# A direct path for the first query stacks, and products of ones on TensorE, at the start of two attention layers

## What is computed

```python
    def _L1_xattn_ref(Q, K, V, Wq, bq, Wk, bk, Wv, bv, Wo, bo):
...
        q = proj(Q, Wq, bq)
        k = proj(K, Wk, bk)
        v = proj(V, Wv, bv)
        scores = jnp.einsum('bhqd,bhkd->bhqk', q, k) / np.sqrt(Dk)
        attn = jax.nn.softmax(scores, axis=-1)
        out = jnp.einsum('bhqk,bhkd->bhqd', attn, v)
        out = out.transpose(0, 2, 1, 3).reshape(B, -1, D)
        return jnp.einsum('bsd,de->bse', out, Wo.T) + bo
...
    x = x + jnp.tanh(g_xattn[1]) * _L1_xattn_ref(_layernorm(x, axis=-1), ctx_1024, ctx_1024, L1_xattn_Wq, L1_xattn_bq, L1_xattn_Wk, L1_xattn_bk, L1_xattn_Wv, L1_xattn_bv, L1_xattn_Wo, L1_xattn_bo)
```

## Time and profile before

| | |
|---|---|
| three timed executions | 1617.97, 1623.83, 1623.98 us; median 1623.83 |
| the profiled execution | 1621.11 us, of which its span 1619.3 us |
| TensorE matmul busy | 1384.8 us, 86% of the span |
| VectorE, ScalarE, GpSimd busy | 861.7, 547.1 and 418.2 us |
| SyncE's DMA queue q1 | 133.89 MB, 28.4% of 16 engines' span |

### The profile page before, as it was taken

The page is one execution under the profiler, slowest core; times in us unless marked ns, Lnnn a source line. Parts: engine busy times, 40 slices in busy tenths (PEclk is TensorE's granted clock), DMA queues, the critical chain, the costliest instruction groups (busy, mean ns, idle before and its releaser), DMA issues. The chain is left out here.

```text
span 1619.3 us, 26329 instructions
## 1 busy us (share of the span) xinstructions
PE 1384.8 (86%) x8869; PEld 865.7 (53%) x8869; DVE 861.7 (53%) x2507; ACT 547.1 (34%) x1291; POOL 418.2 (26%) x729
## 2 busy tenths in 40 slices
PE   5799886995999859896994994756999999999998
PEld 2577663543787636555883773543444444344343
DVE  5577646874676523323663433754455546446425
ACT  2366555652577622223551331430101011011001
POOL 3687501104777100001344123620000000000000
PEclk9699987995799979995776997887999999999999
DMA  6766730004677468000001111232211302202200
GB/s 181 169 153 150 161 83 1 1 1 106 157 170 178 84 244 354 0 1 27 27 27 36 49 55 43 65 117 105 105 51 61 111 19 93 112 1 110 105 7 13
DMA packets 74720, 143.01 MB, mean 88 GB/s; under 512 B 13430, under 2 KB 53878, under 8 KB 64742
## 3 DMA queue, kind: packets, MB, share of 16 engines
q1 hardware_dynamic: 68038, 133.89, 28.4%
q0 software_dynamic: 3296, 6.76, 1.4%
q10 hardware_dynamic: 3264, 0.79, 0.3%
HBM read 99.33 MB, written 41.09 MB: 87 GB/s over the span
## 5 line engine op out<-in xcount | busy, mean ns | idle before, releaser
L2700 DVE TENSOR_TENSOR l3f_weighted_T<-l3f_w_e,l3f_xnT 128x512 f32<-128x512 f32 x128 | 88.4, 691 | 129.7 <-PE psum L2451 114.5
L2451 PE MATMUL psum<-l3f_weighted_T,w_l3f_q 128*128 128x512 f32 x256 | 133.7, 604 | 16.5 <-DVE l3f_weighted_T L2700 14.7
L2451 PE MATMUL psum<-l3f_weighted_T,w_l3f_k 128*128 128x512 f32 x256 | 131.6, 596 | 0.0
L2451 PE MATMUL psum<-l3f_weighted_T,w_l3f_v 128*128 128x512 f32 x256 | 131.3, 594 | 0.0
L2460 PE MATMUL psum<-l3f_weighted_T,w_l3f_o 128*128 128x512 f32 x256 | 124.3, 624 | 1.7 <-DVE l3f_weighted_T L2700 1.7
L2700 DVE TENSOR_TENSOR l3f_weighted_T<-l3f_w_e,l3f_oT 128x512 f32<-128x512 f32 x128 | 88.4, 692 | 57.2 <-PE psum L2460 30.3
L707 DVE TENSOR_REDUCE l1x_minus_max<-psum 128x4 f32<-128x512 f32 x128 | 84.7, 686 | 61.4 <-PE psum L360 60.5
L707 DVE TENSOR_REDUCE l0x_minus_max<-psum 128x4 f32<-128x512 f32 x128 | 84.4, 686 | 38.6 <-PE psum L360 37.9
L111 POOL TENSOR_TENSOR l3f_ln_rstd<-l3f_ln_mean_var,eps 128x4 f32<-128x4 f32 x8 | 2.0, 245 | 355.8 <-DVE l3f_ln_mean_var L104 355.8
L2460 PEld LDWEIGHTS psum<-l3f_weighted_T,w_l3f_o 128*128 128x128 f32 x256 | 39.3, 188 | 82.8 <-DVE l3f_weighted_T L2700 78.1
L2451 PEld LDWEIGHTS psum<-l3f_weighted_T,w_l3f_v 128*128 128x128 f32 x256 | 48.9, 191 | 61.8 <-issue 61.8
(11 more groups left out here) (486 smaller groups left out, 2991.5 us busy)
## 6 DMA issues: line engine op xcount, KB each, us to landing
l3f_w_e<-l3f_weights_scratch SPq DMA_DIRECT2D x32, 1024.0 KB, 4.7
sorted_x<-zeros SPq DMA_DIRECT2D x1, 16896.0 KB, 59.5
l0x_k_stack<-l0x_k_scratch SPq DMA_DIRECT2D x48, 192.0 KB
l0x_q_stack<-l0x_q_scratch SPq DMA_DIRECT2D x48, 192.0 KB
l1x_k_stack<-l1x_k_scratch SPq DMA_DIRECT2D x48, 192.0 KB
l1x_q_stack<-l1x_q_scratch SPq DMA_DIRECT2D x48, 192.0 KB
w_l2f_w<-in_l2f_w SPq DMA_DIRECT2D x2, 2048.0 KB, 13.2
l0x_k_scratch<-l0x_k_parts SPq DMA_DIRECT2D x16, 192.0 KB, 6.4
```

The costliest lines, as they stand in the source:

```text
L2451: ins = pe.matmul(bank[:, :], w[name][:, e, :], xe[:, e % 2, :], start=(e == 0), stop=(e == NE3 - 1))
L2700: dve.tensor_tensor(xe[:, e % 2, :], wE[:, g % 2, e, :], src, ALU.mult).then_inc(s_xe, 1)
```

## The change

The first halves of the q stacks of the groups 0 and 1 no longer pass through DRAM. `lay_straight` copies each part from `parts` straight to its three places in the stack: 9 transfers of 64 KB, each from 128 partitions (512 bytes of each) to 8 partitions, issued as each part is ready. The second halves still take the way over DRAM, and so do all later groups. The load of group 1's first k half moves ahead of its q.

TensorE gets products of ones (`keep_busy`, 512 columns in float32, the result is never read): two at the start of layer 1, four ahead of the first scores, one after each second set of scores, 14 in layer 1 and 12 in layer 0. The projections of the groups 0 and 1 get PSUM banks of their own and another order; turned maxima 1 and 2, the transposes and the q projection of group 2 move into iteration 0 of the loop, and the other engines' lists follow. x and ctx are loaded in eight pieces of 256 KB instead of three and a rest. In the diff the blocks are, in order, helpers, SyncE's list, TensorE's list (the prelude, then iteration j of the loop), GpSimd's, VectorE's, and the pieces of x and ctx.

```diff
+        def banks_of(n, g):
+            return {("k", 1): bankS, ("q", 1): bankT, ("v", 0): bankT}.get((n, g), [bankP0, bankP1])
+        def xn_bank(g):
+            return bankA if g < 2 else bankP1
...
+            def lay_straight(g):
+                for a in range(NPART):
+                    if a < NPART - 1:
+                        links = 4 if rope else 3
+                        sp.wait_ge(s_first if g == 0 else s_split, links + (2 if rope else 1) + 2 * a)
+                    else:
+                        sp.wait_ge(s_parts["q"], g + 1)
+                    for b in range(NPART):
+                        at = (b * NPART + (a - b) % NPART) * HD
+                        sp.dma_start(stack["q"][at:at + HD, g, 0, :, :], parts["q"][:, a, half(0)])\
+                          .then_inc(s_stack["q"][g][0], 16)
...
-            store("q", 0)
-            load("q", 0, 0)
+            lay_straight(0)
+            store("q", 0, (1,))
             load("q", 0, 1)
             if name == "l0x":
                 k.load_x(sp, 3)
-                k.load_ctx(sp, 3)
             for g in range(1, NG):
                 store("k", g)
-                store("q", g)
-                load("k", g, 0)
-                load("q", g, 0)
+                if g == 1:
+                    load("k", g, 0)
+                    lay_straight(g)
+                    store("q", g, (1,))
+                else:
+                    store("q", g)
+                    load("k", g, 0)
+                    load("q", g, 0)
+                if name == "l0x" and g + 2 < NG:
+                    k.load_ctx(sp, g + 2)
+                if name == "l0x" and g + 3 < NG:
+                    k.load_x(sp, g + 3)
                 load("k", g, 1)
                 load("q", g, 1)
...
+            def keep_busy(n):
+                for _ in range(n):
+                    pe.matmul(bankA[:, :], v1[:, 0, 0, 0:HEADS - 1, :].rearrange("p h d -> p (h d)")[:, 0:P],
+                              v1[:, 0, :, :, :].rearrange("p c h d -> p (c h d)")[:, 0:T], start=True, stop=True)
...
-            for g in range(2):
-                project_k(g)
-                turn_xn(g)
-                project_q(g)
-                project_v(g)
-                if g == 0:
-                    pe.matmul(bankM[:, 0:P], bcast(w["bv"][:, 0:1], [P, P]), w["wo"][:, :], start=True, stop=True).then_inc(s_bp, 1)
+            if not rope:
+                pe.wait_ge(s_fill, 4)
+                keep_busy(2)
+            k.wait_weights(pe, name)
+            pe.wait_ge(s_fill, 4)
+            project_k(0)
+            if not rope:
+                project_k(1)
+                project_v(0)
+            turn_xn(0)
+            if rope:
+                project_v(0)
+            project_q(0)
+            turn_xn(1)
+            if rope:
+                project_k(1)
+            project_q(1)
+            project_v(1)
+            pe.matmul(bankM[:, 0:P], bcast(w["bv"][:, 0:1], [P, P]), w["wo"][:, :], start=True, stop=True).then_inc(s_bp, 1)
+            pe.wait_ge(s_out["k"], 2)
+            keep_busy(4)
             for j in range(LEAD):
                 for u in range(4):
                     scores(j, u)
-                if j >= 1:
-                    turn_max(j - 1)
+                    if u % 2:
+                        keep_busy(1)
                 if j == 1:
-                    project_k(2)
-                if j == 2:
-                    turn_xn(2)
-            project_q(2)
+                    turn_max(0)
+            project_k(2)
+            pe.wait_ge(s_out["q"], 2)
...
                 unit(1)
+                if j == 0:
+                    turn_max(1)
...
                 unit(2)
+                if j == 0:
+                    turn_xn(2)
                 unit(3)
+                if j == 0:
+                    turn_max(2)
                 if j + LEAD - 1 < NSEQ:
                     turn_max(j + LEAD - 1)
+                if j == 0:
+                    project_q(2)
...
-            for g in range(3):
-                moments(g)
+            moments(0)
+            moments(1)
             split("k", 1)
+            moments(2)
+            split_max(0)
             split("q", 1)
-            split_max(0)
             split_max(1)
-            moments(3)
             split_max(2)
             split("k", 2)
+            moments(3)
...
             moments(0)
+            moments(1)
             rotate("k", 0)
             split_first("k")
-            moments(1)
...
-    PIECES = (slice(0, T), slice(T, 2 * T), slice(2 * T, 3 * T), slice(3 * T, NSEQ * P))
+    PIECES = tuple(slice(g * T, (g + 1) * T) for g in range(NG))
```

More of the change, by code:

```diff
@@ L256, in heads_attention, with straight @@
         stores = {"k": 1, "q": 2}
+        def straight(n, g, hf):
+            return n == "q" and g < 2 and hf == 0
         def stack_landed(eng, n, g, hf):
-            eng.wait_ge(s_stack[n][g % 2][hf], 16 * loads[n] * (g // 2 + 1))
+            loaded = loads[n] * (g // 2 + 1)
+            if n == "q" and hf == 0:
+                loaded += NPART * NPART - loads["q"]
+            eng.wait_ge(s_stack[n][g % 2][hf], 16 * loaded)
         def parts_stored(eng, n, g, hf):
-            eng.wait_ge(s_stored[n][hf], 16 * stores[n] * (g + 1))
+            if straight(n, g, hf):
+                stack_landed(eng, n, g, hf)
+            else:
+                through = g + 1 if n == "k" or hf == 1 else g - 1
+                eng.wait_ge(s_stored[n][hf], 16 * stores[n] * through)
         block = ctx.enter_context(nc.Block())
@@ L272, in _, with store @@
                          bcast(ones_row[:, 0:HALF].unsqueeze(1), [NPART, 4 * HEADS, HALF])).then_inc(s_ones, 16)
-            def store(n, g):
+            def store(n, g, halves=(0, 1)):
                 sp.wait_ge(s_parts[n], g + 1)
-                for hf in range(2):
+                for hf in halves:
                     to = scratch[n][g % 2, hf].rearrange("a p t -> p a t")
@@ L332, in turn_xn @@
                 pe.wait_ge(s_xn, g + 1)
-                if rope:
+                if g >= 1:
+                    pe.wait_ge(s_xnT, g)
+                if g >= 2 and rope:
                     pe.wait_ge(s_out["k"], g + 1)
                 for c in range(GS):
-                    ins = pe.transpose(bankP1[:, seq(c)], xn[:, c, :], k.ident[:, :])
+                    ins = pe.transpose(xn_bank(g)[:, seq(c)], xn[:, c, :], k.ident[:, :])
                 ins.then_inc(s_xnP, 1)
             def project_q(g):
-                pe.wait_ge(s_out["k"], g + 1)
+                if g == 1:
+                    pe.wait_ge(s_vout, 1)
+                else:
+                    pe.wait_ge(s_out["k"], g + 1)
                 pe.wait_ge(s_xnT, g + 1)
@@ L344, in project_v @@
             def project_v(g):
-                pe.wait_ge(s_out["q"], g + 1)
+                if g >= 1:
+                    pe.wait_ge(s_out["q"], g + 1 if g > 1 else 1)
+                k.wait_ctx(pe, g)
                 for c in range(GS):
-                    ins = pe.matmul(bankP0[:, seq(c)], k.ctxT[:, seq(g * GS + c)], w["wv"][:, :], start=True, stop=True)
+                    ins = pe.matmul(banks_of("v", g)[0][:, seq(c)], k.ctxT[:, seq(g * GS + c)], w["wv"][:, :],
+                                    start=True, stop=True)
                 ins.then_inc(s_proj["v"], 1)
@@ L533, in _ @@
             act.wait_ge(s_fill, 4)
-            for g in range(2):
-                evacuate("k", g)
-                for c in range(GS):
-                    normalise_x(g, c)
-                xnT_out(g)
-                evacuate("q", g)
-                v_out(g)
+            evacuate("k", 0)
+            for c in range(GS):
+                normalise_x(0, c)
+            if not rope:
+                v_out(0)
+            xnT_out(0)
+            evacuate("q", 0)
+            if rope:
+                v_out(0)
+            for c in range(GS):
+                normalise_x(1, c)
+            evacuate("k", 1)
+            xnT_out(1)
+            evacuate("q", 1)
+            v_out(1)
+            max_out(0)
+            max_rows(0)
             for c in range(GS):
                 normalise_x(2, c)
-            max_out(0)
-            max_rows(0)
             evacuate("k", 2)
-            max_out(1)
-            max_rows(1)
-            xnT_out(2)
-            max_out(2)
-            max_rows(2)
-            evacuate("q", 2)
-            normalise_x(3, 0)
             for j in range(NSEQ + 2):
@@ L558, in _ @@
                     exps(j, 1)
+                if j == 0:
+                    max_out(1)
+                    max_rows(1)
                 if j >= 2:
@@ L564, in _ @@
                     exps(j, 2)
+                if j == 0:
+                    xnT_out(2)
                 if c == 3 and t + 3 < NG:
@@ L568, in _ @@
                     exps(j, 3)
+                if j == 0:
+                    max_out(2)
+                    max_rows(2)
                 if j + LEAD - 1 < NSEQ:
@@ L571, in _ @@
```

(9 more changed lines are left out.)

32 lines of the change are left out of this document (16 added, 16 removed).

## The result

The changed kernel takes 1642.0 us, median, against 1623.9: ratio 1.0114, 95% interval 1.0082 to 1.0146. It is slower, and by 18 us where the forecast said 12. One of its four timed executions, 1667.3 us, was a slow one; it is in the median and not in the ratio. The profiled execution has a span of 1637.3 us against 1619.3.

The account below looks back on a forecast made before the run. Bounds: TensorE in the loops (95 and 99% busy), and at each layer's start the moment group 1's four stack halves are in. Layer 0 +0.4 and layer 1 +11.6 make +12.0 on 1621.1 us: 1633, range 1610 to 1648.

Parts of the forecast that it names:

- Price of a straight half: Nine transfers into 8 partitions each, on SyncE's queue, take 8.0 us, by two readings 6.8 to 9.2.
- the row of ones: Profile row of transfers from SBUF into 3 partitions: 24 GB/s, 8.0 per partition, 14% of 16 DMA engines busy.
- First scores: Start of each layer: layer 0's at 36.4 against 36.22, +0.2; layer 1's 5.0 us later.
- The products' charge of 5.0: Head of layer 1: fill and two products of ones ahead of k's projection, charged at 5.0 us.
- Group 1's half: Group 1's straight half, for which iteration 0 waits, lands at 58.6 in layer 0 and 426.2 in layer 1.
- Iteration 1 at 68.0 instead of 67.63: +0.4: Layer 0's loop: iteration 1 starts when sequence 1's maxima land with the loads ahead of them, 0.4 us later.
- +11.6: Layer 1's loop: iteration 1 at 434.3 against 422.70, by the same steps of transfers.
- In the loop the pieces of x and ctx add 1.3 us … nothing: Layer 0's loop: 1.3 us of transfers per 22.6 us group, DMA engines idle 30% of the time, cost nothing.
- (a): Straight halves are cheap, at most 3 us each; iteration 1 10.5 us earlier in layer 0; 1610, faster; chance 0.18.
- (b): Transfers to different partitions overlap, 3 to 6.8 us a half; 1613 to 1628, about 1621, same; chance 0.31.
- (d): The straight half is priced like the ones' transfer as a whole; 1701 us; chance 0.02.
- (c): Products of ones don't raise TensorE's clock; a sequence's scores take 5.5 us instead of 3; 1641; chance 0.09.

Follow-up runs that it names:

- e2: Kernel before with only the straight halves (and the load of group 1's first k half ahead of its q); ratio 1.0110.
- g4: Changed kernel as in e3, and VectorE's statistics of group 1 put back behind the split of group 0's k; ratio 1.0154 to the kernel before.
- e3: Changed kernel without the two products of ones and the wait for GpSimd's fill ahead of layer 1's first k projection; ratio 1.0209 to the kernel before.
- g2: Changed kernel with GpSimd splitting group 1's q ahead of sequence 0's maxima, as before; ratio 1.0191 to the kernel before.
- e1: Changed kernel with the four straight halves sent through DRAM again, the rest kept; ratio 1.0149 to the kernel before.
- g3: Changed kernel with e1's halves through DRAM and g2's GpSimd order together; ratio 1.0182 to the kernel before.
- e6: Changed kernel with group 2's transposes and q projection put back ahead of the loop; ratio 1.0157 to the kernel before.
- h1: Kernel before plus four products of ones a layer in iteration 24, where TensorE waits for group 7's stacks; ratio 0.9988.
- g1: Kernel before with only the eight pieces of x and ctx, loaded one group ahead inside the loop; ratio 1.0015.
- h2: Changed kernel with x and ctx loaded as before, no pieces in the loop; ratio 1.0133 to the kernel before.
- e4: Changed kernel without any products of ones (14 in layer 1, 12 in layer 0); ratio 1.0144 to the kernel before.
- h4: Changed kernel with six parts undone together, those of e1, e3, g4, e6, g2 and h2; ratio 1.0064 to the kernel before.

## Why the prediction was right or wrong

**Price of a straight half: right.** By the bytes that windows of 1 us count in layer 1 (behind k's 1.18 MB come 0.92 MB, the half with the store that runs between its packets), and less 1.3 us for that store, nine took 7.4 us in the changed kernel, 8.4 in e2 and 10.2 in g4. The forecast took 8.0, of 6.8 to 9.2; g4's lies above that. The way to the price holds less well: the prediction read the row of ones as about one busy DMA engine for each partition written, 8 of 16 here, and named few busy engines as a sign; the windows show 0.62 to 0.66 of the 16 busy, so the right size is in part luck. Issuing the nine took SyncE 6.2 us and not 4, which did no harm in layer 0, as k's bytes ended at 27.8 and the issuing at 28.4.

The Trainium skill, page "SBUF — State Buffer", section "Door 1: The DMA port swizzle", gave an estimated 10.8 us. g4's 56 GB/s agree with its two ports of 27.2, the 66 and 78 of e2 do not; whether consecutive transfers overlapped there no run shows. By that estimate the sum would have been 1644, nearer to the 1642.0 than the forecast's 1633, but by luck: nine took 7.4 us, and what the forecast lacked lay elsewhere.

**First scores: right in layer 1 (+4.95 for +5.0), 0.85 us short in layer 0** (37.25 for 36.4), since the store that I set behind the straight half runs between its packets. The products' charge of 5.0 was right in the sum, but not alone: VectorE's statistics, charged at 0.9 in layer 0 and at nothing in layer 1, lay under it with 2.7 (e3, g4): without the products alone the first scores gain 1.5 of the 5.0.

**Group 1's half: right.** 58.82 for 58.6; 425.6 for 426.2 (432.85 less 7.26). The reason given, that the parts are there in time, held only because the straight transfers begin with the first part; g2, e1 and g3 show that GpSimd's order and the buffer of parts hold the other ways.

**The step that failed: "Iteration 1 at 68.0 instead of 67.63: +0.4".** It was 73.44, +5.8. Sequence 1's maxima, which the forecast let end this stretch, were in at 69.6 by the trace's semaphore, 1.6 us later than worked out. The other 3.9 us are TensorE's own list behind the wait for group 1's half: 2.7 us for GpSimd's split of sequence 3's maxima, group 2's q projection, moved into iteration 0, the wait for its rotation, and the v projection that stood there before, with TensorE's work at the low clock. The section on the change names that move, and the prediction gave it no term. e6 takes it away and starts iteration 1 at 70.60, with sequence 1's maxima in at 70.3. In layer 1 transfers and list ended together (maxima in at 443.0, iteration 1 at 443.15), so +11.6 was near +13.2. Two profiles of the same code start layer 0 3.6 us apart (before, h1), so the 5.8 is uncertain by as much; that TensorE's list and not the transfer ended last is read inside one trace.

**"In the loop the pieces of x and ctx add 1.3 us … nothing": wrong.** They cost 2.4 to 11.9 us in the nine profiles that have them. An idle share of 30% over a group did not say that a small transfer is in time, and the late ones cost their wait and a stretch of low clock (g1). At the start the pieces pay: h2, without them, is 8.1 us later there.

**Rivals.** (a) is out: no half took under 7.4 us. (b) is out by the time, and by the price only just, as it ended at 6.8. (d) is out. (c) does not hold as put: the clock did come up (1.00, then 0.99 for the scores). It fell again in the wait for group 1's half, and without the products (e4) nothing is lost that the profiles can tell.

**What makes up the 18.** Two delays at the start that don't add (e1, e2), since both end in the same wait for group 1's stacks and maxima; the list in iteration 0; the pieces. This is read from traces: undoing these parts one at a time did not bring the time back in any run, and with six undone 0.64% stays, whose cause is open.

## What to carry to other kernels

A transfer that saves a round trip was worth nothing here while it held the queue longer than the two that it replaced (7.4 us or more against 4.7); count what is issued behind it, small transfers above all. When work is moved behind a wait, it needs a term of its own: add up the list of the engine from that wait on, at the clock that the wait leaves. Two parts of a change that end in one wait are not told apart by undoing one: do one alone as well.

## What the runs showed of the hardware

After TensorE had done nothing for 4.5 us (before, to 199.0) and 5.6 us (after, to 58.8) its granted clock was 0.50 over the 11 to 13 us shown. Five waits on GpSimd of up to 1.1 us in the regular groups of the kernel before left it at 1.00; waits of 1.1 (h1), 1.2 (after) and 2.8 us (g1) for a late transfer were followed by 0.72, 0.72 and 0.56 over some 6 us. The same nine transfers at the same place ran at 56, 78 and 90 GB/s in three kernels (g4, e2 and the changed kernel, the last with a store among them). Code that is the same differed by 3.6 us in layer 0's start (before, h1). Behind loads that were already issued, sequence 0's 12 KB of maxima, issued at 413.03 in h4, held TensorE until 425.04.
